# A gated attention block in fp32 accuracy: the start of the first group of heads reordered, the gated maximum taken from signed gates, six buffers for the factors of the product, the down weight in four pieces

## The chip, the core and the metric

The kernel runs on one core of a Trainium2 chip. The core has five engines with instruction streams of their own: PE (TensorE, matrix products into PSUM), DVE (VectorE), ACT (ScalarE), POOL (GpSimd) and SP (SyncE, which here issues nearly all DMAs). They meet only through semaphores. The metric is the device time of one execution in microseconds (us); lower is better.

## What is computed

x is (4, 1024, 512), the context of the same shape, all in fp32. The block is an attention of the normalized x over the context with 16 heads of 32 columns, then a feed-forward part whose activations and weights are quantized and dequantized (qdq). Cut to what matters:

```
q = rope(layernorm(x)); k = rope(ctx); v = ctx
scores = q k^T / sqrt(32) + slope[h] * (key - query)
x = x + tanh(g_xattn) * softmax(scores) v
h = act_qdq(layernorm(x))                       # 16 bits, one scale for the whole tensor
up = act_qdq(h @ lpbq(w_up).T); gate = act_qdq(h @ lpbq(w_gate).T)
gate = act_qdq(gate * u16_qdq(sigmoid(gate)))
x = x + tanh(g_ffn) * (act_qdq(gate * up) @ lpbq(w_down).T)
act_qdq(a): s = max|a| / 32767; round(a / s) * s
```

Each act_qdq needs the largest absolute value of the whole tensor before the first element can be quantized. So there are five such points: x, gate, gated gate, up, product.

## The kernel before, in words

**Attention.** The 64 pairs of batch and head are worked in 16 groups of four heads (p). A group has two halves of 512 queries (hf), and a half has 8 key tiles. `Step(g)` says what every engine does in step g; step g = 8 hf + kt. Row maxima run eleven steps ahead of the scores (`LEAD` 3 plus 8): a step takes two of them, each two 512-column matmuls on PE (L866) and one DVE reduction over 1024 columns (L1215). They need QA[p % 2] and KA[p % 2], the stacks of the high and low halves of queries and keys in 16 bits, with the position bias in rows 96 to 99. A stack is made so: ACT normalizes x (L1011), DVE or POOL applies rope, PE turns the tile (`turn`), ACT writes the high half `hi` (L1017), DVE the low half `lo` (L1229), SP stores both into DRAM (`store_parts`) and loads them from there in the layout of the stack (`load_stack`). For group 0 this stands ahead of everything. DVE first fills rows 96 to 127 of all four stacks (L1238, L1239), then takes the statistics of the first eight tiles of x (L1203). The eighth of them uses the buffer of the first (`NXL` 7), so its load waits for the first tile's statistics.

**Gate projection.** PE multiplies x_hl (high and low halves of the quantized x, one chunk `cp` of 1024 rows after the other) by Wg in 48 units `12 cp + ot` of 24 matmuls, 5.18 us each (the distance of two evictions). ACT evicts a unit into one of three buffers `ev` (L1111), DVE takes its largest absolute value (`largest`, L1451), SP stores it to DRAM. Beside that DVE and ACT prepare the x tiles of the next chunk (`low_x`, then SP's transposition `turn_x`, L655) and quantize the up and down weights (`wround`, `wsplit`, `wstore` in TILE_JOBS).

**Up projection.** 48 units with Wu, whose pieces SP loads by transposition, two for each four units (`load_wu`, some 2.7 us of SP for the two). Beside each unit ACT and DVE work through the gate chunks that `GATE_PLAN` gives to the step. Of the first kind there are 48: SP loads the chunk from DRAM (`load_gate`, three buffers gt), ACT quantizes it into gq (L1145) and takes the sigmoid (L1136), DVE rounds the sigmoid (L1487) and takes the largest |gq| * sigmoid (L1508); |gq| is written first into gab, by ACT (L1151) or DVE (L1505). Then the global maximum (`global_max`) gives the second scale. The second kind (`gated`: sigmoid again on ACT, rounding and product on DVE, L1493) rewrites gq. `LATE` of these are left for later. The down weight Wd[0] is loaded by one transposition in the 32nd step (L778).

**Products.** After the global maximum of up come 48 products of 1024 columns: SP loads up (`uf`, four buffers), ACT writes |up| quantized into uq (three buffers, L1163), ACT or DVE writes |gq| into pab (two buffers, L1171 on ACT for 33 of 48, L1534 on DVE for 15), DVE takes the largest product (L1537). The gated chunks that are left stand partly ahead of the products, partly between them. Wd[1] is loaded by one transposition behind the load for product 29 (L815). Then comes the down projection (L991), 1152 matmuls.

In the names of the profile, `ol` and `oh` are the memory in which pab and the products' operands lie.

Of the kernel before, what the change touches and what calls it, by code (L numbers as in the profile page):

```python
# [32 lines left out]
LATE = 14  # L33
# [71 lines left out]
class Step:  # L105


    def __init__(self, g):
# [11 lines left out]
        if w == 8 and 0 <= p and p + 2 < NQ:  # L120
            self.turn = (p + 2, 0)
        elif w == 0 and 0 <= p and p + 1 < NQ:
            self.turn = (p + 1, 1)
        elif g == -3:
            self.turn = (1, 0)
# [24 lines left out]
        elif g == -2:  # L150
# [79 lines left out]

def score_no(hf, kt, h):
# [32 lines left out]
ALL = 9  # L264
ALL_NO = {n: ALL * (k + 1) for k, n in enumerate(("w0", "x_row", "w1", "w2", "g_row", "h_row", "u_row", "o_row"))}
# [22 lines left out]
class Kernel:  # L288


    def __init__(self, nc, ctx, x, ctx_in, gx, gf, wg, wu, wd, cos_d, sin_d, id_d, bias_d, out):
# [35 lines left out]
        self.red = A("red", [128, 10], F32)  # L327
# [5 lines left out]
        self.mxg = A("mxg", [128, 48], F32)  # L333
# [66 lines left out]
        self.gab = [A(f"gab{i}", [128, GW], I16) for i in range(2)]  # L400
# [14 lines left out]
        self.prt = [self.ol[0][:, 4 * i:4 * i + 4, :].rearrange("p a n -> p (a n)").bitcast(F32) for i in range(2)]  # L415
        self.pab = [self.ol[1][:, 2 * i:2 * i + 2, :].rearrange("p a n -> p (a n)").bitcast(I16) for i in range(2)]
# [10 lines left out]
        self.d_st = [sem(f"d_st{i}") for i in range(2)]  # L427
        self.d_crow = [sem(f"d_crow{i}") for i in range(2)]
# [24 lines left out]
        self.a_sig, self.a_gab, self.a_uabs = sem("a_sig"), sem("a_gab"), sem("a_uabs")  # L453
# [8 lines left out]
        self.v_mx, self.v_sgq, self.v_gab, self.v_gmax = sem("v_mx"), sem("v_sgq"), sem("v_gab"), sem("v_gmax")  # L462
# [4 lines left out]
        self.g_ropek = sem("g_ropek")  # L467
# [41 lines left out]
def columns(p):  # L509
# [8 lines left out]
         "g_row", "g_v", "g_s", "g_r0", "g_r", "f2",  # L518
# [18 lines left out]
GAB_ON_ACT = [n % 12 in (0, 2, 5, 7, 10) for n in range(48)]  # L537
# [3 lines left out]
def gab_no(n):  # L541

    return sum(GAB_ON_ACT[i] == GAB_ON_ACT[n] for i in range(n + 1))

# [16 lines left out]
def sync_program(e, K):  # L561
# [19 lines left out]
    def store_parts(p, w):  # L581
        e.wait_ge(K.a_hi, turn_no(p, w, 1))
        if p >= 2:
            e.wait_ge(K.d_st[p % 2], 112 * (p // 2))
# [7 lines left out]
    def load_stack(p, w):  # L592
        if p >= 2:
            e.wait_ge(K.pe_score, score_no(2 * (p - 2) + 1, 7, 3))
        e.wait_ge(K.d_part[w], 32 * p + 32)
        if p == 0 and w == 0:
            e.wait_ge(K.v_aux, 4)
# [6 lines left out]
        if w == 0:  # L604
            if p == 0:
                e.wait_ge(K.d_bias, 48)
# [1189 lines left out]
```

## Time and profile before

| | us |
|---|---|
| median of 3 runs | 1931.48 (1930.20 to 1932.11) |
| the profiled execution | 1931.96 |
| its span, first to last instruction | 1930.2 |
| PE busy | 1681.3 (87%) |
| DVE busy | 1482.4 (77%) |
| ACT busy | 1189.2 (62%) |
| POOL busy | 809.6 (42%) |
| mean granted TensorE clock | 0.957 of full |

The chain of work that ended last spends 29% of the span on PE, nearly all in the two projection loops and the down projection. In the page's 40 slices (48 us each) PE is full from the third to the 32nd but for the 22nd, empty in the first and the 33rd and 34th, and full again to the end. A row of a timeline shows start, duration, engine, line, operation, and the idle time of that engine just before it with what ended it. A duration with xN goes from the start of the first of N instructions to the end of the last.

### The profile page before, as it was taken

The numbers are of one execution on the slowest core, as the hardware profiler recorded it, in microseconds if no ns is written. First come the engines' busy times: TensorE is split into PE (matmuls) and PEld (weight loads), VectorE is DVE, ScalarE is ACT, GpSimd is POOL, SyncE is SP. The second block draws the span as 40 slices with busy tenths as digits, with TensorE's granted clock in tenths as the row PEclk, the third lists the DMA queues.
The fourth block names the chain that finished last, engine by engine and source line by source line (L and its number), as shares of the span: only waits on it lengthen the run. The fifth ranks groups of instructions, "written<-read, shape, count | busy, mean of one in ns | idle before, by whom it ended". The sixth has DMA issues, their size and how long they took to land. (4 is left out here: it accounts for less than half of the span.)

```text
span 1930.2 us, 24973 instructions
## 1 busy us (share of the span) xinstructions
PE 1681.3 (87%) x8888; PEld 631.8 (33%) x8888; DVE 1482.4 (77%) x2113; ACT 1189.2 (62%) x1911; POOL 809.6 (42%) x442
## 2 busy tenths in 40 slices
PE   0899999999999999999975999999998900399999
PEld 0222333333333333333222444444443400044444
DVE  5889888888888887888855676549999998854451
ACT  2366677777777777776652332349996588854440
POOL 3488888978889888887620010200000000000000
PEclk9999999999999999999997999999999955699999
DMA  5478776657776667665356898759885268655452
GB/s 150 92 189 195 170 180 155 162 130 163 170 176 153 158 146 175 165 149 132 80 161 163 246 260 253 218 173 270 259 263 158 104 206 246 228 182 173 164 164 76
DMA packets 234396, 340.54 MB, mean 176 GB/s; under 512 B 73984, under 2 KB 153216, under 8 KB 226016
## 3 DMA queue, kind: packets, MB, share of 16 engines
q1 hardware_dynamic: 225344, 273.94, 48.2%
q0 software_dynamic: 8928, 65.02, 16.9%
q8 instruction: 70, 1.15, 0.2%
q14 instruction: 54, 0.44, 0.1%
HBM read 165.61 MB, written 93.45 MB: 134 GB/s over the span
## 5 line engine op out<-in xcount | busy, mean ns | idle before, releaser
L1033 ACT ACTIVATE P<-quad 128x512 f32<-128x512 f32 x1024 | 557.4, 599 | 223.1 <-PE quad L878 218.6
L1215 DVE TENSOR_REDUCE cm<-quad 128x1 f16<-128x1024 f32 x512 | 601.3, 1216 | 98.3 <-PE quad L866 97.1
L1721 POOL TENSOR_TENSOR Ps<-P,P 128x2048 f32<-128x2048 f32 x93 | 422.8, 4546 | 145.0 <-ACT P L1033 144.9
L878 PE MATMUL quad<-QA,KA 101*128 101x512 f16 x1024 | 352.4, 385 | 7.8 <-ACT P L1033 6.7
L866 PE MATMUL quad<-KA,QA 100*128 100x512 f16 x1024 | 328.9, 392 | 32.9 <-issue 12.9
L991 PE MATMUL quad<-Wd,oh 128*128 128x512 f16 x768 | 231.6, 382 | 131.8 <-DVE ol L1559 131.7
L914 PE MATMUL quad<-P,cg 128*32 128x512 f32 x2048 | 273.6, 606 | 3.6 <-ACT numT L1064 0.6
L960 PE MATMUL quad<-x_hl,Wg 128*128 128x512 f16 x1152 | 251.5, 382 | 22.2 <-DMA x_hl<-xs 22.2
L960 PE MATMUL quad<-x_hl,Wu 128*128 128x512 f16 x1152 | 251.5, 381 | 6.4 <-DMA Wu<-wt_scratch 6.4
L1111 ACT ACTIVATE ev<-quad 128x1024 f32<-128x1024 f32 x96 | 97.5, 1016 | 201.4 <-PE quad L960 196.6
L1451 DVE TENSOR_REDUCE mxt<-ev 128x1 f32<-128x1024 f32 x96 | 116.9, 1217 | 95.9 <-ACT ev L1111 95.5
L878 PEld LDWEIGHTS quad<-QA,KA 101*128 101x128 f16 x1024 | 85.9, 97 | 299.7 <-ACT P L1033 209.2
L960 PEld LDWEIGHTS quad<-x_hl,Wg 128*128 128x128 f16 x1152 | 113.2, 98 | 160.3 <-issue 26.1
L960 PEld LDWEIGHTS quad<-x_hl,Wu 128*128 128x128 f16 x1152 | 113.0, 98 | 144.7 <-DMA Wu<-wt_scratch 7.4
L866 PEld LDWEIGHTS quad<-KA,QA 100*128 100x128 f16 x1024 | 98.6, 98 | 180.1 <-DVE cm L1215 41.2
L991 PEld LDWEIGHTS quad<-Wd,oh 128*128 128x128 f16 x768 | 75.4, 98 | 227.8 <-issue 130.9
L991 PE MATMUL quad<-Wd,ol 128*128 128x512 f16 x384 | 146.5, 382 | 0.0
L1697 POOL TENSOR_TENSOR wq<-wl,wsc 128x512 f32<-128x512 f32 x36 | 37.9, 1052 | 218.8 <-DVE wl L1326 218.8
L1136 ACT ACTIVATE sgm<-gq,qs 128x1024 f32<-128x1024 int16 x96 | 109.3, 1145 | 26.5 <-DVE sgq L1487 24.0
L1581 DVE SCALAR_TENSOR_TENSOR xr<-quad,qs,xr 128x512 f32<-128x512 f32 x32 | 24.0, 751 | 122.6 <-PE quad L991 122.6
L944 PE MATMUL quad<-Ps,ones 128*32 128x512 f32 x776 | 101.0, 592 | 1.8 <-DMA Ps<-P 1.5
L1180 ACT ACTIVATE uq<-uf,qs 128x512 int16<-128x512 f32 x96 | 68.2, 711 | 53.0 <-DMA uf<-up_scratch 51.5
(140 smaller groups left out, 1841.1 us busy)
## 6 DMA issues: line engine op xcount, KB each, us to landing
Ps<-P POOLq DMA_DIRECT2D x62, 1024.0 KB, 8.1
gate_scratch<-ev SPq DMA_DIRECT2D x48, 512.0 KB, 3.0
gt<-gate_scratch SPq DMA_DIRECT2D x48, 512.0 KB, 5.7
up_scratch<-ev SPq DMA_DIRECT2D x48, 512.0 KB, 3.1
uf<-up_scratch SPq DMA_DIRECT2D x48, 512.0 KB, 4.8
uf<-up_scratch SPq DMA_DIRECT2D x96, 256.0 KB, 3.8
KA<-part_scratch SPq DMA_DIRECT2D x48, 256.0 KB
QA<-part_scratch SPq DMA_DIRECT2D x48, 256.0 KB
```

What stands on the lines that cost most here:

```text
L866: mm = e.matmul(K.bank(use, c), K.QA[p % 2][0:100, qc, h, q0:q0 + 128], K.KA[p % 2][0:100, h, 512 * c:512 * c + 512], start=True, stop=True)
L878: e.matmul(K.score[h % 2], K.KA[p % 2][0:101, h, 128 * kt:128 * kt + 128], K.QA[p % 2][0:101, qc, h, :], start=True, stop=True).then_inc(K ...
L914: mm = e.matmul(K.num[32 * h:32 * h + 32, :], K.cg[p % 3][:, kt, 32 * h:32 * h + 32], K.Pb[before.g % NP][:, h, :], start=kt == 0, stop=kt ...
L944: mm = e.matmul(K.den[32 * h:32 * h + 32, :], K.ones[:, :], K.Ps[n % 2 if hf == NHALF - 1 else n][:, h, :], start=n == 0, stop=n == (3 if ...
L960: mm = e.matmul(K.quad[z][:, 512 * h:512 * h + 512], W(part, c), K.x_hl[:, x, c0:c0 + 512], start=n == 0, stop=n == 11)
L991: mm = e.matmul(ps, o[k][:, ot, sl], K.Wd[r][:, ot, :], start=m == 0, stop=m == 3 * OT - 1)
L1033: e.activation(K.Pb[pb][:, h, :], K.score[h % 2], ACT.Exp, scale=SCALE / (QPOW * KPOW)).then_inc(K.a_exp, 1)
L1111: e.activation(K.ev[k % NEV][:, :], K.quad[k % 4][:, :], ACT.Copy).then_inc(K.a_ev, 1)
L1136: e.activation(K.sgm[n % NSG][:, :], view(n), ACT.Sigmoid, scale=sg).then_inc(K.a_sig, 1)
L1215: e.tensor_reduce(cm[:, u:u + 1], K.quad[UNIT["max", hm, u] % 2][:, :], AX.X, ALU.max).then_inc(K.v_max, 1)
L1451: e.tensor_reduce(K.mxt[:, col:col + 1], K.ev[k % NEV][:, :], AX.X, ALU.max, apply_absolute_value=True).then_inc(K.v_mx, 1)
L1721: e.tensor_tensor(K.Ps[n][:, :, :], K.Pb[(st.g - 1) % NP][:, :, :], K.Pb[st.g % NP][:, :, :], ALU.add).then_inc(K.g_sum, 1)
```

## The change

Four edits:

1. **Start.** Rows 96 to 127 of KA[0] and QA[0] are filled by ACT, those of KA[1] and QA[1] by DVE later, behind the low halves of keys and queries. The key turn of group 0 is split on ACT and DVE ahead of the normalization. Its halves don't go through DRAM: 12 DMAs of 32 partitions copy keys from hi and lo into KA[0], 12 more the queries, with a semaphore for each head. The turn and the store of group 1's queries stand four steps earlier (g = -7 and -6 instead of -3 and -2).
2. **Gated maximum.** gab and its 48 copies go. DVE multiplies gq itself with scale -1, so that it finds the largest product of the negative gates; the positive side is taken from the largest signed gate, which a second reduction per unit of the gate projection gives (`highest`) with a second global maximum `s_row`. GATE_PLAN puts the 48 gates into 25 steps instead of 28 and 40 of the gated chunks instead of 34 into steps 26 to 46; `LATE` is 8 instead of 14.
3. **Products.** Six buffers for pab and for |up| (`uqa`) instead of two and three. ACT's copy for product n + 5 is issued behind the operand of product n.
4. **Down weight.** Wd[0] is loaded in four pieces, one in each of the last four groups of four units, behind the second store of the group; Wd[1] in four pieces at the place where the one load stood.

```diff
-LATE = 14
+LATE = 8
+NUA = 6
...
-        elif g == -3:
+        elif g == -7:
             self.turn = (1, 0)
...
-        elif g == -2:
+        elif g == -6:
             self.store_parts = (1, 0)
...
-        until = 48 * step // 28 if step <= 28 else 48 + (48 - LATE) * (step - 28) // 20
+        until = 48 * step // 25 if step <= 25 else 48 + (48 - LATE) * min(step - 25, 21) // 21
...
-    return range(48 - LATE, 52 - LATE), {n: 52 - LATE + n // 2 for n in range(48) if n % 2 == 1 and 52 - LATE + n // 2 < 48}
+    return range(48 - LATE, 50 - LATE), {2 * i + 1: 50 - LATE + i for i in range(LATE - 2)}
...
+    def first_keys():
+        e.wait_ge(K.v_lo, 2)
+        for h in range(4):
+            for n, src in enumerate((K.hi[1], K.lo[1], K.hi[1])):
+                e.dma_start(K.KA[0][32 * n:32 * n + 32, h, :], src[32 * h:32 * h + 32, :]).then_inc(K.d_first_k, 16)
+        e.wait_ge(K.a_aux, 2)
+        e.wait_ge(K.d_bias, 48)
...
+    def first_queries():
+        e.wait_ge(K.v_lo, 4)
+        for h in range(4):
+            for n, src in enumerate((K.hi[0], K.hi[0], K.lo[0])):
+                dst = K.QA[0][32 * n:32 * n + 32, :, h, :]
+                e.dma_start(dst, src[32 * h:32 * h + 32, :].rearrange("d (c t) -> d c t", c=2)).then_inc(K.d_first_q[h], 16)
...
-    store_parts(0, 1)
-    store_parts(0, 0)
-    load_stack(0, 1)
-    load_stack(0, 0)
+    first_keys()
+    first_queries()
...
+    def load_wd(part, j):
...
+        rows = slice(128 * j, 128 * j + 128)
+        e.dma_start_transpose(K.Wd[part][:, :, rows], K.wt_d[2][part][rows, :]).then_inc(K.d_Wd, 16)
...
+    e.wait_ge(K.a_tg, 1)
+    for rows, value in ((K.KA[0][96:128, :, :], -1.0), (K.QA[0][96:128, :, :, :].rearrange("p c h t -> p (c h) t"), QPOW * KPOW)):
+        some = K.tg[96:128, 0:1].to_broadcast([32, rows.shape[1] * rows.shape[2]]).rearrange("p (a t) -> p a t", a=rows.shape[1])
+        e.activation(rows, some, ACT.Copy, scale=0.0, bias=value).then_inc(K.a_aux, 1)
+    turned(0, 1, 0)
+    turned(0, 1, 1)
     normalize(0, 0, 8)
...
+    def gate_abs(n):
+        if PAB_ON_ACT[n]:
+            e.wait_ge(K.v_g2, n + 1)
+            if n >= NUA:
+                e.wait_ge(K.v_pmax, n - NUA + 1)
+            e.activation(K.pab[n % NUA], view(n), ACT.Abs).then_inc(K.a_pab, 1)
...
-        e.activation(K.uq[n % NUQ][:, :], K.uf[uf_uses % NUF][:, :], ACT.Abs, scale=ru).then_inc(K.a_uabs, 1)
+        e.activation(K.uqa[n % NUA], K.uf[uf_uses % NUF][:, :], ACT.Abs, scale=ru).then_inc(K.a_uabs, 1)
         uf_uses += 1
         if n in beside:
             sigmoid(beside[n], 48 + beside[n])
...
+        if n + NUA - 1 < 48:
+            gate_abs(n + NUA - 1)
...
+    def highest(k, col):
+
+        e.tensor_reduce(K.mxs[:, col:col + 1], K.ev[k % NEV][:, :], AX.X, ALU.max).then_inc(K.v_mx, 1)
...
-                    e.tensor_tensor_reduce(out=K.sgm[k][:, :], in0=K.gab[z][:, :], in1=K.sgq[k][:, :], scale=1.0, scalar=0.0, op0=ALU.mult,
+
+                    e.tensor_tensor_reduce(out=K.sgm[k][:, :], in0=view(n), in1=K.sgq[k][:, :], scale=-1.0, scalar=0.0, op0=ALU.mult,
```

**What moved on SP at the start.** Before, behind the load of the second group's x:

```order
L675 DMA bias_scratch<-biash_100 32x1024
L587 DMA part_scratch<-hi_144 128x1024
L589 DMA part_scratch<-lo_146 128x1024
L587 DMA part_scratch<-hi_143 128x2x512
L589 DMA part_scratch<-lo_145 128x2x512
L603 DMA KA_91<-part_scratch 32x4x1024 x3
L603 DMA QA_89<-part_scratch 32x8x512 x3
L608 DMA KA_91<-bias_scratch 4x4096
```

Now, at the same place; the copies of the other heads are alike and stand between:

```order
L702 DMA bias_scratch<-biash_104 32x1024
L624 DMA KA_95<-hi_148 32x1024
L624 DMA KA_95<-lo_150 32x1024
...
L628 DMA KA_95<-bias_scratch 4x4096
L635 DMA QA_93<-hi_147 32x2x512 x2
L635 DMA QA_93<-lo_149 32x2x512
```

The four stores into part_scratch are gone, and each head has three copies of its own for keys and three for queries.

**What moved on ACT in the up projection.** Four steps before, each begun by an eviction into ev:

```order
L1111 ACTIVATE ev_165<-quad 128x1024
L1145 ACTIVATE gq<-gt_172,qs 128x1024
L1136 ACTIVATE sgm_174<-gq,qs 128x1024
L1151 ACTIVATE gab_178<-gq 128x1024
L1111 ACTIVATE ev_163<-quad 128x1024
L1145 ACTIVATE gq<-gt_170,qs 128x1024
L1136 ACTIVATE sgm_173<-gq,qs 128x1024
L1145 ACTIVATE gq<-gt_171,qs 128x1024
L1136 ACTIVATE sgm_174<-gq,qs 128x1024
L1151 ACTIVATE gab_178<-gq 128x1024
L1111 ACTIVATE ev_164<-quad 128x1024
```

Now:

```order
L1158 ACTIVATE ev_169<-quad 128x1024
L1192 ACTIVATE gq<-gt_176,qs 128x1024
L1183 ACTIVATE sgm_177<-gq,qs 128x1024
L1192 ACTIVATE gq<-gt_174,qs 128x1024
L1183 ACTIVATE sgm_178<-gq,qs 128x1024
L1158 ACTIVATE ev_167<-quad 128x1024
```

The copies gab are gone, and nearly every step has two gates (gq, sgm), where before steps with one and with two alternated.

**What moved on ACT in the products.** Before, at the first products (uq is |up|, ol is |gq|, sgm a gated chunk's sigmoid):

```order
L1163 ACTIVATE uq_185<-uf_181,qs 128x1024
L1171 ACTIVATE ol_191<-gq 128x1024
L1163 ACTIVATE uq_186<-uf_182,qs 128x1024
L1136 ACTIVATE sgm_173<-gq,qs 128x1024
L1163 ACTIVATE uq_187<-uf_183,qs 128x1024
L1171 ACTIVATE ol_191<-gq 128x1024
```

Now (|up| is oh):

```order
L1222 ACTIVATE oh_190<-uf_186,qs 128x1024
L1183 ACTIVATE sgm_178<-gq,qs 128x1024
L1208 ACTIVATE ol_192<-gq 128x1024
L1222 ACTIVATE oh_190<-uf_183,qs 128x1024
L1208 ACTIVATE ol_192<-gq 128x1024
L1222 ACTIVATE oh_190<-uf_184,qs 128x1024
```

The copy of |gq| stands behind the sigmoid, and it is that of five products later.

## Rows read from the trace of the kernel before

**Rows 1.** Window: us, busy and (instructions) by engine, PEclk, DMA share, GB/s.

```profile
1300.00:1400.00 100.00, 100.00 (x465) 45.34 (x463) 96.43 (x127) 95.07 (x92) 0.00 (x0) 1.00 0.88 262
```

**Rows 2.** Timeline of the start, all engines.

```profile
9.09 1.05 ACT L1047 ACTIVATE biash<-bias 32x1024 f16<-32x1024 f32 x1 [2.70 <-DMA bias<-in_alibi_dram]
...
14.48 3.47 DVE L1239 MEMSET QA<- 32x4096 f16 x1 [0.80 <-issue]
...
18.03 0.67 DVE L1203 BATCH_NORM_STATS2 st<-xl 128x6 f32<-128x512 f32 x1
...
24.40 1.18 DVE L1245 TENSOR_TENSOR biash<-bias,biash 32x1024 f16<-32x1024 f32 x1
...
29.44 3.18 ACT L1011 ACTIVATE xn<-xg,nm,rs 128x128 f32<-128x128 f32 x8 [19.30 <-POOL nm L1637]
...
39.11 0.69 DVE L1229 SCALAR_TENSOR_TENSOR lo<-quad,hi 128x512 f16<-128x512 f32 x1 [0.16 <-ACT hi L1017]
...
52.44 10.65 DVE L1215 TENSOR_REDUCE cm<-quad 128x1 f16<-128x1024 f32 x9 [12.63 <-PE quad L866]
```

**Rows 3.** DMA issues, 0 to 60 us: count, KB each, median us to landing.

```profile
xl<-in_x_dram SPq DMA_DIRECT2D x8, 256.0 KB, 6.7
...
part_scratch<-hi SPq DMA_DIRECT2D x2, 256.0 KB, 2.1
```

**Rows 4.** Gate projection: DVE's reduction by line, one unit's window, SP's timeline.

```profile
L1451 DVE TENSOR_REDUCE mxt<-ev 128x1 f32<-128x1024 f32 x47 | 57.3, 1220 | 88.5 <-ACT ev L1111 88.5
...
1127.48:1132.72 5.24, 5.24 (x26) 2.36 (x25) 4.45 (x8) 2.13 (x3) 1.05 (x1) 1.00 1.05 247
...
1156.73 1.84 SPq L655 DMA_TRANSPOSE x_hl<-xs  x1
```

**Rows 5.** Up projection: timeline; waits on and landing of the gate loads.

```profile
1284.54 45.70 PE L960 MATMUL quad<-x_hl,Wu 128*128 128x512 f16 x211
...
1290.50 1.02 ACT L1111 ACTIVATE ev<-quad 128x1024 f32<-128x1024 f32 x1 [4.74 <-DVE qs L1423]
...
1302.63 1.00 ACT L1111 ACTIVATE ev<-quad 128x1024 f32<-128x1024 f32 x1
...
1304.07 1.21 SPq L761 DMA_DIRECT2D gt<-gate_scratch  x2
...
1305.91 1.13 ACT L1145 ACTIVATE gq<-gt,qs 128x1024 int16<-128x1024 f32 x1
...
1308.14 1.00 ACT L1111 ACTIVATE ev<-quad 128x1024 f32<-128x1024 f32 x1
...
  DMA gt<-gate_scratch: 6.6, 9
...
DMA to landing us min/median/max: 4.4/5.7/6.7
```

**Rows 6.** Timeline of the later up projection, DVE and PE.

```profile
1455.42 0.19 DVE L1409 TENSOR_REDUCE red<-mxg 128x1 f32<-128x48 f32 x1
...
1464.57 1.28 DVE L1493 SCALAR_TENSOR_TENSOR gq<-sgq,qs,gq 128x1024 int16<-128x1024 uint16 x1
...
1469.54 1.28 DVE L1493 SCALAR_TENSOR_TENSOR gq<-sgq,qs,gq 128x1024 int16<-128x1024 uint16 x1
...
1477.94 7.33 PE L960 MATMUL quad<-x_hl,Wu 128*128 128x512 f16 x23 [5.38 <-DMA Wu<-wt_scratch]
...
1548.54 0.19 DVE L1409 TENSOR_REDUCE red<-mxt 128x1 f32<-128x48 f32 x1
```

**Rows 7.** Timeline of the products, DVE and SP.

```profile
1559.56 1.22 DVE L1537 CUSTOM_DVE_ANT_0 ol<-uq,ol 128x1024 f32<-128x1024 int16 x1
...
1616.50 1.22 DVE L1537 CUSTOM_DVE_ANT_0 ol<-uq,ol 128x1024 f32<-128x1024 int16 x1
...
1617.36 8.65 SPq L815 DMA_TRANSPOSE Wd<-wt_scratch  x1
...
1665.94 0.20 DVE L1409 TENSOR_REDUCE red<-mxt 128x1 f32<-128x48 f32 x1
```

More of the change, by code:

```diff
@@ L536, with mx_no @@
 GATE_PLAN = gate_plan()
-GAB_ON_ACT = [n % 12 in (0, 2, 5, 7, 10) for n in range(48)]
 PAB_ON_ACT = [n % 16 * 11 % 16 < 11 for n in range(48)]
-def gab_no(n):
-    return sum(GAB_ON_ACT[i] == GAB_ON_ACT[n] for i in range(n + 1))
+def mx_no(k):
+    return 2 * k + 2 if k < 48 else 49 + k
 def pab_no(n):
@@ L761, in load_gate @@
         e.dma_start(K.gt[n % NGT][:, :], K.gate_d[ot, :, GW * cp:GW * cp + GW]).then_inc(K.d_gt[n % NGT], 16)
+    def load_wd(part, j):
+        if part == j == 0:
+            e.wait_ge(K.a_gq, 48)
+            for h in range(2):
+                for i in range(2):
+                    e.wait_ge(K.d_wh[h][i], 16 * 18)
+        rows = slice(128 * j, 128 * j + 128)
+        e.dma_start_transpose(K.Wd[part][:, :, rows], K.wt_d[2][part][rows, :]).then_inc(K.d_Wd, 16)
     load_gate(0)
@@ L772, in sync_program @@
                     load_gate(n + 2)
[L773 to L778 removed]
+            if cp == 1 and ot >= 8:
+                load_wd(0, ot - 8)
     uf_uses = [0]
@@ L814, in sync_program @@
             e.wait_ge(K.v_g2, 48)
-            e.dma_start_transpose(K.Wd[1][:, :, :], K.wt_d[2][1]).then_inc(K.d_Wd, 16)
+            for j in range(4):
+                load_wd(1, j)
     for n in range(NUF - 1):
@@ L1014, in turned @@
         e.wait_ge(K.pe_turn, turn_no(p, w, half))
-        if p > 0 and half == 0:
-            e.wait_ge(K.d_part[w], 32 * p)
+        if p == 1 and half == 0:
+            if w:
+                e.wait_ge(K.d_first_k, 208)
+            else:
+                for h in range(4):
+                    e.wait_ge(K.d_first_q[h], 48)
+        elif p > 1 and half == 0:
+            e.wait_ge(K.d_part[w], 32 * p - 32)
         e.activation(K.hi[w][:, 512 * half:512 * half + 512], K.bank(("turn", p, w), half), ACT.Copy, scale=(QPOW, KPOW)[w]).then_inc(K.a_hi, 1)
@@ L1047, in scalar_program @@
     e.activation(K.biash[0][:, :], K.bias[:, :], ACT.Copy).then_inc(K.a_bias, 1)
+    e.wait_ge(K.a_tg, 1)
[4 more added lines that the diff above has]
+    turned(0, 1, 1)
     normalize(0, 0, 8)
-    for w in (1, 0):
-        for half in range(2):
-            turned(0, w, half)
+    turned(0, 0, 0)
+    turned(0, 0, 1)
     for st in STEPS:
@@ L1156, in scalar_program @@
         sigmoid(n, 48 + n)
+    e.wait_ge(K.pe_prj, 96)
+    for n in range(NUA - 1):
+        gate_abs(n)
     e.wait_ge(K.v_q, Q_NO["u_r"])
@@ L1226, in low_part @@
         e.wait_ge(K.a_hi, turn_no(p, w, half))
-        if p > 0 and half == 0:
-            e.wait_ge(K.d_part[w], 32 * p)
+        if p == 1 and half == 0:
+            if w:
+                e.wait_ge(K.d_first_k, 208)
+            else:
+                for h in range(4):
+                    e.wait_ge(K.d_first_q[h], 48)
+        elif p > 1 and half == 0:
+            e.wait_ge(K.d_part[w], 32 * p - 32)
         e.scalar_tensor_tensor(K.lo[w][:, c], K.bank(("turn", p, w), half), (QPOW, KPOW)[w], K.hi[w][:, c], ALU.mult, ALU.subtract).then_inc(K.v_lo, 1)
@@ L1259, in vector_program @@
     e.tensor_tensor(K.t1[0][:, :, :], K.t1[0][:, :, :], K.t2[:, :, :], ALU.add).then_inc(K.v_rope0, 1)
-    for w in (1, 0):
-        for half in range(2):
-            low_part(0, w, half)
+    low_part(0, 0, 0)
+    low_part(0, 0, 1)
+    e.memset(K.QA[1][96:128, :, :, :], QPOW * KPOW).then_inc(K.v_aux, 1)
     def everywhere(out, column, name):
```

115 lines of the change are left out of this document (60 added, 55 removed).

## The prediction

> **What bounds the kernel now.** I read first the busy time of all engines in windows, then the timeline of the places that the change touches, in the order of the program.
>
> From 100 us to 1542 us TensorE is the bound but for short gaps. In the up projection ScalarE and VectorE are close behind it: from 1300 to 1400 us PE is busy 100 of 100 us, DVE 96.4 and ACT 95.1 [rows 1]. Two stretches have no TensorE work to hide in. One is the start: the first row maximum is taken at 52.44 us after 12.6 us in which DVE waited for it [rows 2]. The other is the product stage, from the global maximum of the up projection at 1548.54 [rows 6] to that of the products at 1665.94 [rows 7], 117.4 us, in which DVE is the fullest engine. What is saved at the start moves everything behind it; so does what is saved in the product stage. In between a saving counts only as far as the engine that is late next allows.
>
> **Part 1, the start.** Now the chain is: four fills by DVE of 3.47 us each, the last from 14.48; statistics of eight x tiles from 18.03, done at 24.4; nine small operations on POOL; eight normalizations on ACT at 29.44; rope, turn, split, whose last half ends at 39.11 + 0.69 = 39.80; stores to DRAM; loads of KA and QA from there; first maximum at 52.44 [rows 2].
>
> The fills leave the head of DVE's queue: two go to ACT, two behind other work. ACT ends its bias copy at 10.1 (1.05 us for 1024 columns [rows 2]); an estimate from that row for two fills of 4096 columns is 2 x 4.2 = 8.4 us, until 18.6, and ACT isn't needed by this chain before the key turn at about 19. The statistics can follow the arrival of the tiles: the eighth tile's load waits for the first tile's statistics, which moves from 18.7 to about 12, and a tile lands 6.7 us after issue [rows 3]. So the statistics end at about 18.3 (bounds: 16.5, where the other loads have drained; 20.5, if this one comes last behind all) in place of 24.4. Everything up to the last split follows at the distances it has now: 39.8 - 6.1 = 33.7. In it the key split (1.3 us) and one fill (3.5) that now stand on DVE ahead of rope hide behind POOL and ACT: DVE is free at about 25, rope starts at 26.6. What would uncover them is statistics that end 1.6 us earlier still.
>
> Then the trip through DRAM goes: instead of stores, three large loads each and 12.6 us, there are 12 small transfers for the keys, issued at 21 to 26, and 12 for the queries. Only the first head's three count: 3 issues of 0.4, landing 2.1 us after issue as the stores of hi do [rows 3], 1.0 for the matmuls: 33.7 + 1.2 + 2.1 + 1.0 = 38.0. The other heads are due every 4 x 1.18 us and come every 1.3. The last fill on DVE ends at 33.7 + 3.5 + 0.8 = 38.0: just hidden. So the first maximum comes at 38.0 instead of 52.44: **-14.4 us** (bounds -9 to -16; the far end takes 6.7 us for a landing, as the x tiles have). The second group's turn stands four steps earlier, behind ten maxima at about 50; POOL has its rope ready at 36 + 7.3 = 43, so it costs there what it costs now. I expect the rest of attention to move as a block.
>
> A page speaks against it: the Trainium skill, "SBUF — State Buffer", section "Door 1: The DMA port swizzle", says that a transfer on 32 partitions reaches 8 of the 16 ports, half the rate, and no row here shows such a transfer of this size. By its 436 GB/s the first head's 192 KB would take 0.9 us instead of 0.45, and the sum would be -13.9 instead of -14.4.
>
> **Part 2, the gate projection.** It gains 48 reductions on DVE of 1.22 us [rows 4] in units of 5.18 us of TensorE. Where the weights of the up projection and the x tiles meet, seven units in a row hold 4.45 us of DVE work [rows 4]; with 1.2 more that is 5.65, 0.47 too much each, 3.3 us of lag after seven. The eviction doesn't feel it, its buffer is three units deep. The last x tile of the third chunk does: its low half and the split of the weights behind it come 3.3 + 1.2 us later, at 1157.5. SP stores that split, issues two weight loads (1.9) and a projection (0.4) before it can issue the tile's transposition, which stands at 1156.73 now [rows 4] and goes to about 1160.2: 3.5 late, and TensorE takes the chunk 3.6 us after it now without a wait, so I give it no slack. The same place a chunk later has one load instead of two: 1.8 late. Sum **+5** (bounds 0, if landings leave slack, to +9, if TensorE comes back at 1.2 GHz, as after the 5.4 us gap at 1477.94, where 23 matmuls took 7.3 us [rows 6]).
>
> **Part 3, the up projection.** The first eviction waits for the gate scale, 1.2 later behind the 48th new reduction: 1290.5 [rows 5] to 1291.7; the second maximum (2.5 us) comes behind it and is hidden. The copies of the absolute gate go: 28 on DVE, 20 on ACT. The plan now puts 48 gates in 25 steps instead of 28. On ACT a step with two gates is 0.9 for the eviction and 2 x 2.2 (1305.91 to 1308.14 [rows 5]): 5.35, near TensorE's 5.18. But a loop stands over it. The load of a gate is issued behind the eviction two steps ahead of the next one: from 1302.63 to 1304.07, 1.44 us, then 5.7 us to landing (4.4 to 6.7; the ones that ACT waited for are nearer to 5.9) [rows 5], then two gates, 4.4: 11.8 us for two steps, against 10.4 of TensorE. Twelve such pairs, less 2.2 twice at the two steps with one gate, are 137 us: step 25 at 1428.8. Two gates more (7.2) and a reduction (1.2), and the gated maximum is looked for at 1437.2 instead of 1455.42 [rows 6]. Its chain is 3.4 us, with the three operations on the top value 4.0. Then 40 gated chunks and 22 reductions follow on DVE. Two chunks and one reduction take 4.97 (1464.57 to 1469.54 [rows 6]): 20 x 4.97 + 2 x 1.2 = 101.8. End: 1437.2 + 4.0 + 101.8 = 1543.0 instead of 1548.54: **-5.6 us**. TensorE could be done by 1284.5 [rows 5] + 48 x 5.18 = 1533.2, with 2.5 for evicting and reducing 1536; so DVE is late next. The gap of 5.38 us at 1477.94, where SP put the whole down weight ahead of a piece of the up weight [rows 6], goes, since a quarter now stands behind a store with 20 us to spare; but it frees only TensorE, and isn't counted again. A lag of ACT over about 11 us at a fourth step makes TensorE wait for the next weight; by the sum above the lag is 10 to 12 there, so 0 to 3 us of waits, which DVE hides. Bounds: landings of 5.3 give TensorE's limit, -13; of 6.7, 12 x 0.8 more, +4.
>
> **Part 4, the products.** Two gated chunks instead of four stand ahead of the first product: -3.9. Six instead of ten stand among the products. Now the 24 products from 1559.56 to 1616.50 take 56.9 us [rows 7], DVE without a gap. With the change DVE's own work in the first twelve is 12 x 1.15 + 4 x 1.26 + 6 x 1.92 = 30.4, but the six buffers do not free ACT: it now makes the copy for product n + 5 right behind the operand of n, and that copy's buffer is free only when product n - 1 is done. Behind it stand the next operand and sigmoid, for which DVE waits. That serial piece is 1.0 + 1.0 + 1.1 on ACT, 0.7 + 1.2 + 1.2 on DVE, 6.2 us and hand-overs, for two products, where ACT makes the copy, and 4.2 to 5 where DVE does. I take 5.7 a pair, 34 us, and 12 x 1.8 for the next twelve: 56 against 56.9, -1. From the 24th on ACT bounds both, with 1.7 a product; the stall behind the second down weight (SP busy 8.65 us [rows 7]) stays, since the four pieces follow each other with no load between: one piece is three up weight pieces (1.3 each) less what is fixed, about 2.3, 9.2 in all, +0.6. Sum **-4** (bounds -12, if the operands run free as DVE's own work allows, to +2).
>
> **Sum.** -14.4 + 5 - 5.6 - 4 = -19.0. Against the profiled execution's own 1931.96 us (span 1930.2) this is 1913.0; the median of the runs stands 0.5 below that execution, so I say 1912.5.
>
> **Rivals.** *TensorE's limit*: the gate loads land sooner than DVE needs, and the up projection gives -13: 1905. For it: landings go down to 4.4. Against: nine of 48 gates already wait for their load, at 1.7 a step [rows 5]. The Trainium skill, "DMA: Bandwidth & Descriptors", section "Anatomy of one DMA", gives about 2.0 us plus bytes by 436 GB/s, 3.2 us for these 512 KB, by which this rival would be the outcome; the trace has 5.7 beside other transfers, and that I use. *Small transfers are slow*: the query pieces land like the x tiles and the start gives -8: 1919. *The products run free*: -12 there, 1904.5. *The new reductions drag*: more lag in the gate projection, clock lost, +12 instead of +5: 1919.5. *The change doesn't do what it says*: six buffers bring nothing; this is in my forecast. *Slower than before*: the tighter plan makes the gate loads collide with the stores of the up projection. Each us of landing costs 12 in the first 25 steps; from 7.5 us all of the gain is gone, at 8.4 the kernel stands at 1942. Against: 6.7 is the longest now, and bytes per us rise only by a tenth.
>
> **Chances.** Forecast (1907 to 1917) 0.5; TensorE's limit 0.15; slow small transfers 0.12; reductions drag 0.1; products free 0.1; slower 0.03. The range 1901 to 1923 leaves out the last and the rest of the far bounds. Less than 0.2% (3.9 us) can't be told from no change; to end there two of the parts must fail at once: 0.03. Faster 0.94, slower 0.03.
>
> **What would show it.** The first reduction of a score tile at about 38 us. In the gate projection TensorE waiting at the third and fourth chunk for x_hl. In the up projection ACT waiting for the gate loads in most steps, 11.6 to 12 us per two steps, and the gated maximum near 1437, counted from the same start of that stage. DVE without a gap from there. In the product stage DVE waiting for ACT among the first twelve. Wrong it would be if part 1's shift does not reach the end of attention, or if the landings move by over 0.7 us.

## The result

The changed kernel takes 1908.78 us (median of 4 runs, 1905.94 to 1910.37), the kernel before 1931.80 (4 runs, 1930.20 to 1933.05). The ratio is 0.988, 95% interval 0.9863 to 0.9897: 23.0 us faster, where 19.0 was forecast. The profiled execution of the changed kernel took 1908.31 us, its span is 1906.5.

Cut at the same instructions, the two profiles differ as follows (us). The first five rows add up to the span.

| stage, from ... to ... | before | after | difference | forecast |
|---|---|---|---|---|
| start, to the first row maximum | 52.4 | 38.3 | -14.1 | -14.4 |
| attention, to the first matmul of the gate projection | 980.7 | 980.8 | 0 | 0 |
| gate projection, to the first matmul with Wu | 251.4 | 253.7 | +2.3 | +5 |
| up projection, to its global maximum | 264.0 | 255.6 | -8.4 | -5.6 |
| products, to their global maximum; then the down projection | 117.4; 264.3 | 113.9; 264.2 | -3.5; 0 | -4; 0 |
| of the up projection: to the gated maximum | 170.9 | 150.3 | -20.6 | -18.2 |

The start, timeline of the changed kernel, against [rows 2]:

```profile
10.24 3.61 ACT L1093 ACTIVATE KA<-tg 32x4096 f16<-32x4096 f32 x1
10.42 0.69 DVE L1259 BATCH_NORM_STATS2 st<-xl 128x6 f32<-128x512 f32 x1 [9.50 <-DMA xl<-in_x_dram]
...
18.16 1.18 DVE L1304 TENSOR_TENSOR biash<-bias,biash 32x1024 f16<-32x1024 f32 x1
...
32.87 0.69 DVE L1291 SCALAR_TENSOR_TENSOR lo<-quad,hi 128x512 f16<-128x512 f32 x1 [0.16 <-ACT hi L1058]
33.59 1.32 SPq L635 DMA_DIRECT2D QA<-hi  x2
...
34.95 0.60 SPq L635 DMA_DIRECT2D QA<-lo  x1
...
37.27 1.86 PE L901 MATMUL quad<-KA,QA 100*128 100x512 f16 x4 [5.07 <-DMA QA<-lo]
...
38.32 2.36 DVE L1271 TENSOR_REDUCE cm<-quad 128x1 f16<-128x1024 f32 x2 [0.38 <-PE quad L901]
```

The statistics end 6.2 us earlier (18.16 for 24.40), the last split ends at 33.56 for 39.80, and from there the first row maximum takes 4.8 us in place of 12.6.

The gate projection: the 30 us that end 0.15 us behind the start of the third chunk's last transposition as a window (busy and count of PE, PEld, DVE, ACT, POOL; PEclk, DMA share, GB/s), first in the kernel before, then in the changed one:

```profile
1126.88:1156.88 30.00, 30.00 (x141) 13.60 (x139) 23.31 (x38) 11.68 (x16) 5.24 (x5) 1.00 0.94 264
...
1115.08:1145.08 30.00, 30.00 (x140) 13.58 (x139) 29.68 (x43) 11.99 (x16) 5.24 (x5) 1.00 0.88 248
```

SP's and PE's timelines of the changed kernel, against [rows 4]:

```profile
1144.93 1.77 SPq L682 DMA_TRANSPOSE x_hl<-xs  x1
...
1150.46 62.32 PE L995 MATMUL quad<-x_hl,Wg 128*128 128x512 f16 x288 [1.31 <-DMA x_hl<-xs]
1213.19 57.14 PE L995 MATMUL quad<-x_hl,Wg 128*128 128x512 f16 x264 [0.41 <-DMA x_hl<-xs]
```

DVE is busy 29.7 of these 30 us; in the kernel before it was 23.3. TensorE waits twice, at the third and the fourth chunk; in the kernel before it waits for nothing in the whole stage.

The up projection: the window of [rows 1] (its start lies 27 us behind the stage's start, and there 15), PE's and DVE's timelines, and the loads of the gates, against [rows 5, 6]:

```profile
1300.00:1400.00 100.00, 100.00 (x465) 45.35 (x464) 87.12 (x122) 92.56 (x88) 0.00 (x0) 1.00 0.97 288
```

```profile
1272.76 27.57 PE L995 MATMUL quad<-x_hl,Wu 128*128 128x512 f16 x127
...
1423.08 0.20 DVE L1471 TENSOR_REDUCE red<-mxg 128x1 f32<-128x49 f32 x1
...
1528.40 0.20 DVE L1471 TENSOR_REDUCE red<-mxt 128x1 f32<-128x48 f32 x1
```

```profile
  DMA gt<-gate_scratch: 7.0, 11
...
DMA to landing us min/median/max: 4.5/5.5/7.1
```

DVE is busy 87 of 100 us in place of 96 (the copies of the absolute gate are gone), and TensorE waits for nothing in this profile of the stage. From the gated maximum to the end of the stage DVE is busy 103.4 of 105.3 us: it is late, not TensorE, whose last matmul of the stage starts at 1521.2.

The products, timeline and ACT's two groups of the stage (out<-in, count | busy, mean ns | idle before, releaser), against [rows 7]:

```profile
1535.58 1.22 DVE L1608 CUSTOM_DVE_ANT_0 ol<-oh,ol 128x1024 f32<-128x1024 int16 x1
...
1592.55 1.23 DVE L1608 CUSTOM_DVE_ANT_0 ol<-oh,ol 128x1024 f32<-128x1024 int16 x1 [0.24 <-issue]
...
1593.85 9.99 SPq L795 DMA_TRANSPOSE Wd<-wt_scratch  x4
...
1642.30 0.20 DVE L1471 TENSOR_REDUCE red<-mxt 128x1 f32<-128x48 f32 x1
```

```profile
L1222 ACT ACTIVATE oh<-uf,qs 128x1024 int16<-128x1024 f32 x48 | 53.6, 1135 | 12.5 <-DMA uf<-up_scratch 9.5 <-DVE qs L1485 3.0
L1208 ACT ACTIVATE ol<-gq 128x1024 int16<-128x1024 int16 x33 | 34.4, 1048 | 12.4 <-DVE mxt L1608 12.2
```

The first product comes 7.2 us after the stage's start, where it was 11.0. The next 24 take 57.0 us in place of 56.9. The copies of |gq| on ACT (L1208) waited 12.2 us for a product.

### The profile page after: what moved, and what is told of

Its sections match the earlier page's. It is cut to its first block and busy times, and to the rows that moved or that the text cites. A ratio compares the mean times of both kernels' runs of the same rounds, so it can differ in the third digit from the quotient of the medians.

```text
span 1906.5 us, 24960 instructions
## 1 busy us (share of the span) xinstructions
PE 1679.1 (88%) x8888; PEld 631.9 (33%) x8888; DVE 1502.7 (79%) x2143; ACT 1182.9 (62%) x1895; POOL 809.8 (42%) x442
```

## The experiments

Each kernel was timed against the kernel before on the same chip. A stage's length comes from the kernel's one profile. "Up" is the up projection to its global maximum, "products" the stage behind it, "tail" the time from TensorE's last matmul with Wu to the maximum of the products (the loads of up values can't begin before that matmul).

| kernel | median us | ratio (95% interval) | gate proj. | gated max. | up | products | tail |
|---|---|---|---|---|---|---|---|
| before | 1931.8 | | 251.4 | 170.9 | 264.0 | 117.4 | 123.9 |
| changed | 1908.8 | 0.988 (0.9863 to 0.9897) | 253.7 | 150.3 | 255.6 | 113.9 | 121.1 |
| e1_start | 1918.0 | 0.9942 (0.9928 to 0.9957) | 251.4 | 172.0 | 264.5 | 116.4 | 122.8 |
| e2_fills | 1925.1 | 0.9976 (0.9964 to 0.9987) | 251.4 | 169.9 | 262.3 | 115.6 | 122.0 |
| e3_no_signed | 1906.9 | 0.988 (0.9863 to 0.9896) | 251.3 | 152.7 | 258.0 | 115.1 | 120.8 |
| e4_ahead4 | 1903.2 | 0.9871 (0.9852 to 0.989) | 253.8 | 155.3 | 260.6 | 106.2 | 114.5 |
| e5_spread | 1904.0 | 0.9857 (0.9842 to 0.9872) | 253.2 | 152.6 | 257.9 | 108.5 | 116.0 |
| e6_ngt4 | 1905.3 | 0.9869 (0.9855 to 0.9884) | 253.6 | 141.9 | 251.2 | 116.7 | 119.4 |
| e7_wd0 | 1907.1 | 0.9878 (0.9862 to 0.9895) | 253.6 | 152.4 | 257.6 | 113.9 | 119.7 |
| e8_old_buffers | 1904.7 | 0.9862 (0.9847 to 0.9877) | 253.0 | 155.2 | 260.4 | 108.0 | 115.7 |
| e9_combo | 1891.1 | 0.9801 (0.9784 to 0.9819) | 253.9 | 141.8 | 251.2 | 102.6 | 105.3 |
| e10_late4 | 1888.9 | 0.9789 (0.9774 to 0.9803) | 253.1 | 142.9 | 257.0 | 96.8 | 105.4 |
| e11_early | 1890.1 | 0.9797 (0.978 to 0.9813) | 253.9 | 143.0 | 257.1 | 94.9 | 103.5 |
| e12_late6 | 1890.7 | 0.9786 (0.9772 to 0.98) | 253.6 | 143.4 | 253.7 | 100.0 | 105.2 |

Two columns measure how far one profile can be trusted. The up projection has the same code in the changed kernel, e4, e5, e7 and e8, and takes 255.6, 260.6, 257.9, 257.6 and 260.4: what varies is how soon the gate loads land. ACT waited for them 7.0, 12.0, 8.9, 9.1 and 11.8 us, and each length less its wait is 248.5 to 249.0. Attention takes 977.9 to 981.7 in all fourteen profiles. So a difference of 2 us in a stage is read only where the stage itself repeats, as the gate projection and the down projection (264.2 to 264.6) do.

The whole times say less. The interval of the changed kernel overlaps those of e3 to e8, so each of these six differs from it only in the length of its stages. Of the kernels that start from the changed one, e9 to e12 alone are faster than it as a whole.

### The start alone

```diff
-    store_parts(0, 1)
-    store_parts(0, 0)
-    load_stack(0, 1)
-    load_stack(0, 0)
+    first_keys()
+    first_queries()
...
-        elif g == -3:
+        elif g == -7:
             self.turn = (1, 0)
```

This one has the whole first edit (the fills, the order of steps, the direct copies, the turn), and nothing else of the change.

> The kernel before with the reordering of the first group's steps alone (fills, key and query steps, direct copies in place of the trip through DRAM, the second group's turn four steps earlier). The whole of it is computed. Theory (attention moves as a block): the first row maximum at 38.3 us, the first matmul of the gate projection at 1033.16 - 14.1 = 1019.1, every later stage as long as before, so 1931.8 - 14.1 = 1917.7. Rival (the shift is partly eaten by work that did not move, POOL's or a transfer's): the first maximum at 38.3, but the gate projection starts later than 1021, and the whole gains less than 12.

Measured: 1917.95 us, the first maximum at 38.3, the gate projection's first matmul at 1020.0, later stages as before. Against the kernel before on this chip (1930.42) that is 12.5 us by the medians, 8.3 to 13.9 by the ratio's interval, whose end lies just short of 14.1; the spans of the two profiles differ by 13.6, since attention took 0.9 longer in this one, which is within its scatter. No later stage took anything of it systematically: what is saved at the start is saved at the end, within 1 to 3 us.

### The fills and the order without the direct copies

```diff
-        e.memset(K.KA[i][96:128, :, :], -1.0).then_inc(K.v_aux, 1)
-        e.memset(K.QA[i][96:128, :, :, :], QPOW * KPOW).then_inc(K.v_aux, 1)
...
+        e.activation(rows, some, ACT.Copy, scale=0.0, bias=value).then_inc(K.a_aux, 1)
```

> The kernel before with only the fills and the order of steps of the first group changed; the trip through DRAM and the second group's turn stay as before. Theory (the two gains of the start are separate): the last split ends at 33.6 in place of 39.8, the trip takes its 12.6 us as before, the first maximum at 46.2, and the whole is 1931.8 - 6.2 = 1925.6. Rival (the trip was set by something that did not move, such as the bias rows or the loads of other tiles on the same queue): the first maximum later than 48, and a gain under 4.5.

Measured: 1925.06 us, 5.4 below the kernel before on the same chip (2.5 to 7.0 by the interval). Its timeline at the same place as that of the changed kernel above:

```profile
33.66 0.37 SPq L589 DMA_DIRECT2D part_scratch<-lo  x1
...
45.16 1.86 PE L868 MATMUL quad<-KA,QA 100*128 100x512 f16 x4 [12.89 <-issue]
...
46.21 4.71 DVE L1223 TENSOR_REDUCE cm<-quad 128x1 f16<-128x1024 f32 x4 [8.20 <-PE quad L868]
```

The last split ends at 33.63, the trip takes its 12.6 us, the maximum comes at 46.2. So the 14.1 us are two gains that add: 6.2 from the head of DVE's queue, 7.9 from the trip.

### No signed reductions

```diff
-            highest(u, 4 * ot + cp)
...
-    global_max(K.mxs[:, :], "s_row")
+    global_max(K.mxt[:, :], "s_row")
```

> The changed kernel without its 48 signed reductions in the gate projection; the top gate is taken from the largest absolute value instead, so the scale of the gated values can differ. The gate projection takes 253.7 us in the changed kernel and 251.4 in the one before. Theory (the reductions hold back the split of the last x tiles of the third and fourth chunk): without them the two short waits for x_hl go, the stage takes 251.4 again, and the whole is 1908.8 - 2.3 = 1906.5. Rival (the waits come from transfers, which stand otherwise since the stage starts earlier): they stay, the stage takes 253 or more, and the whole is within 0.7 of the changed kernel.

Measured: the gate projection takes 251.3 us again, and the whole 1906.88; the ratio is that of the changed kernel, 0.988, so the whole time can't show the 2.3 us, and the stage does. The ten kernels with the reductions stand at 253.0 to 253.9, the four without them (before, e1 and e2 too) at 251.3 to 251.4. So some 2.3 us are the reductions' price. Its timeline shows no wait at the third and the fourth chunk any more. (A wait of 1.18 us for x_hl that it does show stands at 1022.95, five microseconds into the stage, and others have the like.)

### Copies four products ahead

```diff
-    for n in range(NUA - 1):
+    for n in range(NUA - 2):
         gate_abs(n)
...
-        if n + NUA - 1 < 48:
-            gate_abs(n + NUA - 1)
+        if n + NUA - 2 < 48:
+            gate_abs(n + NUA - 2)
```

> The changed kernel with one number changed: ScalarE makes the absolute copy four products ahead instead of five, so the buffer it writes is that of product n - 2, not of the product just being computed. Theory (the copy waits for the product before it, 12.2 us of ACT in the stage, and six buffers bring nothing for that reason): the waits go, the stage of 113.9 us (from the global maximum of the up projection to that of the products) takes about 105, and the whole is about 1900. Rival (the loads of the up values or DVE's own work set the pace there): ACT's waits move to the loads, the stage takes 111 or more and the whole 1906 or more.

The chain that this experiment is to break, timeline of the changed kernel, seventh and eighth product:

```profile
1551.68 1.22 DVE L1608 CUSTOM_DVE_ANT_0 ol<-oh,ol 128x1024 f32<-128x1024 int16 x1
1551.86 1.06 ACT L1208 ACTIVATE ol<-gq 128x1024 int16<-128x1024 int16 x1 [2.24 <-DVE mxt L1608]
1552.82 1.13 ACT L1222 ACTIVATE oh<-uf,qs 128x1024 int16<-128x1024 f32 x1
...
1553.86 1.13 ACT L1183 ACTIVATE sgm<-gq,qs 128x1024 f32<-128x1024 int16 x1
...
1555.02 0.69 DVE L1555 TENSOR_SCALAR sgq<-sgm 128x1024 uint16<-128x1024 f32 x1 [2.11 <-ACT sgm L1183]
1555.75 1.28 DVE L1561 SCALAR_TENSOR_TENSOR gq<-sgq,qs,gq 128x1024 int16<-128x1024 uint16 x1
...
1558.21 1.22 DVE L1608 CUSTOM_DVE_ANT_0 ol<-oh,ol 128x1024 f32<-128x1024 int16 x1
```

ACT's copy waits 2.24 us until a product is done; the next operand and the sigmoid stand behind it; DVE waits 2.11 for the sigmoid. From one product to the next 6.5 us pass in which each engine waits for the other once; with the copies four ahead the same distance is 4.3. This is the longest of three such places in the first twelve products; the other two cost 0.9 us each. In the kernel with the copies four ahead ACT's group of copies reads:

```profile
L1208 ACT ACTIVATE ol<-gq 128x1024 int16<-128x1024 int16 x33 | 34.3, 1044 | 4.7 <-DVE mxt L1608 4.7
```

Measured: the wait falls from 12.2 to 4.7 us, the stage takes 106.2 in place of 113.9 (105 expected), the first 24 products 50.3 us in place of 57.0. The whole is 1903.20, 3 above the expectation, and the ratio, 0.9871, can't be told from the changed kernel's 0.988. Part of the reason may be what the profile has: the longest up projection of its kind, 260.6, in which ACT waited 12.0 us for gate loads. The rival, which had the loads as the limit, is out: ACT's wait for them went from 9.5 to 10.1 us only.

### The second down weight in pieces that are apart

```diff
-        if n == 26:
-            e.wait_ge(K.v_g2, 48)
-            for j in range(4):
-                load_wd(1, j)
+        if n in (20, 24, 28, 32):
+            if n == 20:
+                e.wait_ge(K.v_g2, 48)
+            load_wd(1, (n - 20) // 4)
```

> The changed kernel with the four pieces of the second down weight put four products apart (behind the loads at products 20, 24, 28 and 32) instead of all at product 26. Theory (the block of 10 us on SP leaves ACT without its up values for about 8 us, and one piece of 2.5 us fits between loads that run three ahead): no wait over 2 us for a load in the stage, which takes 113.9 - 6 = 108, the whole about 1903. Rival (ACT's wait for its own copy buffer takes back what the loads give): the stage takes 111 or more. If the pieces themselves disturb the loads of the up values, it takes 114 or more.

Measured: 108.5 us for the stage, 1903.98 for the whole. ACT's operands:

```profile
L1222 ACT ACTIVATE oh<-uf,qs 128x1024 int16<-128x1024 f32 x48 | 53.5, 1135 | 7.4 <-DMA uf<-up_scratch 4.4 <-DVE qs L1485 3.0
```

The wait for loads falls from 9.5 to 4.4 us, the stage by 5.4. Cutting the load in four, as the change does, gives nothing here as long as the pieces follow each other: SP is busy with them 9.99 us in place of 8.65 [rows 7], and ACT's longest wait for an up value behind them is 6.5 us in place of 6.0. Only apart do they pay.

### Four gate buffers

```diff
-NGT, NSG = 3, 2
+NGT, NSG = 4, 2
...
-                if n + 2 < 48:
-                    load_gate(n + 2)
+                if n + 3 < 48:
+                    load_gate(n + 3)
```

> The changed kernel with four buffers for the gate values instead of three and their loads issued three ahead. Theory (the loop eviction, store, load, landing, two gates sets the first 25 steps of the up projection): ACT's waits for gates (7.0 us in 11 times, in the sister runs up to 12.0) shrink under 3; ACT's own 5.35 a step sets the pace, the gated maximum comes 138 to 142 us after the stage's start instead of 150 to 155, and the stage ends near TensorE's limit, at 251 to 252 instead of 255.6 to 260.6: the whole about 1904. Rival (ACT and DVE hold each other by the two sigmoid buffers, loads only fill the slack): the gated maximum stays above 148.

DVE's timeline, and the loads of the gates:

```profile
1412.80 0.20 DVE L1472 TENSOR_REDUCE red<-mxg 128x1 f32<-128x49 f32 x1
```

```profile
DMA to landing us min/median/max: 4.8/6.3/8.1
```

Measured: no wait of ACT for a gate load is left, though the loads land later than before (6.3 for 5.5 us). The gated maximum comes 141.9 us after the stage's start, the stage takes 251.2, 2.7 behind TensorE's last matmul. That is the rival "TensorE's limit" of the prediction, made to happen: the loop over landings had set the pace. But the whole gains less than the 4.4 us of this stage, since the products start earlier and the loads of up values don't: their stage is 2.8 longer, and the tail only 1.7 shorter.

### The first down weight in one piece

```diff
-            if cp == 1 and ot >= 8:
-                load_wd(0, ot - 8)
+            if 4 * ot + cp + 1 == 32:
...
+                e.dma_start_transpose(K.Wd[0][:, :, :], K.wt_d[2][0]).then_inc(K.d_Wd, 16)
```

> The changed kernel with the first down weight loaded in one piece at step 32 of the up projection, as before the change; the second stays in four pieces. Theory (its gap frees only TensorE, since DVE is late next): TensorE waits about 5 us for a piece of the up weight, its last matmul of the stage comes up to 5 later than 248.4 us after the start, the global maximum of the up projection stays within 1.5 of 255.6 to 260.6, and the whole within 1.5 of the changed kernel. Rival (TensorE's end carries through): the maximum 4 to 5 later, the whole 1913.

Measured: up 257.6 us, whole 1907.14: within 1.7 us of the changed kernel's whole, and no slower (ratios 0.9878 and 0.988). The price on TensorE was missed:

```profile
1448.76 6.63 SPq L812 DMA_TRANSPOSE Wd<-wt_scratch  x1
...
1459.58 62.33 PE L999 MATMUL quad<-x_hl,Wu 128*128 128x512 f16 x288 [1.70 <-DMA Wu<-wt_scratch]
```

TensorE waits 1.70 us and not 5.38 [rows 6]. SP spends 6.63 us on the weight in both, but here begins at 1448.76, 9.1 before TensorE would have needed the piece of Wu; before the change it began at 1467.14, 5.4 ahead of that. So the four pieces of the first down weight bring nothing that can be measured.

### The products with the buffers of before

```diff
-        if n + NUA - 1 < 48:
-            gate_abs(n + NUA - 1)
+        if PAB_ON_ACT[n]:
+            e.wait_ge(K.v_g2, n + 1)
+            if n >= 2:
+                e.wait_ge(K.v_pmax, n - 1)
+            e.activation(K.pab[n % 2], view(n), ACT.Abs).then_inc(K.a_pab, 1)
```

> The changed kernel with the product stage's buffers and order of copies as before the change (two for the copy of the absolute gated value, made behind its own operand, three for the operand), everything else as changed, with 8 late chunks. Theory (six buffers bring nothing, the 3.5 us gained in this stage come from the fewer late chunks): the stage takes 113 to 115 us, as the changed kernel's 113.9 and 115.1. Rival (the six buffers carry the gain): 117 or more.

ACT's copies of |gq|:

```profile
L1219 ACT ACTIVATE ol<-gq 128x1024 int16<-128x1024 int16 x33 | 34.5, 1044 | 3.3 <-DVE mxt L1598 3.3
```

Measured: 108.0 us for the stage and 1904.72 for the whole. Neither expectation holds. The six buffers as the change uses them don't bring nothing, they cost 5.9 us of the stage, and without them the stage is 9.4 shorter than before (117.4 to 108.0). These 9.4 are the fewer late chunks, and whatever the four pieces of the second weight do to them. With two buffers the copy made beside product n waits for product n - 2, 3.3 us in all; with six and made five ahead, the copy that stands there waits for n - 1, 12.2 us. So the price is that of the lookahead and not of the buffers: with the same six and the copies four ahead (e4) the stage takes 106.2, 1.8 less than with two, a difference that is too small to be read from one profile each.

### Together, and the last late chunks

e9_combo has the edits of e4, e5 and e6 at once.

> The changed kernel with the three edits together: copies four products ahead, the second down weight in pieces four products apart, four gate buffers. Theory (the three take away different waits and add): the up projection from its first matmul to its global maximum 251 to 252 us, the product stage 113.9 - 7.7 - 5.4 = 101, plus 3 because the loads of the up values can't start before TensorE ends: 104, the whole 1908.8 - 4 - 10 = 1895. Rival (one resource, DVE's or ACT's own work, stands behind both waits of the product stage): the stage takes 106 or more, as with the copies alone, and the whole is 1899 or more.

Measured: products 102.6, up 251.2, whole 1891.06, ratio 0.9801: the three add. The kernel before took 1929.0 on this chip, so the ratio is the fair measure: it is worth 38.4 us of 1931.8, where 36.8 were expected. The next one changes the plan too:

```diff
-LATE = 8
+LATE = 4
...
-        until = 48 * step // 25 if step <= 25 else 48 + (48 - LATE) * min(step - 25, 21) // 21
+        until = 2 * step if step <= 24 else 48 + (48 - LATE) * min(step - 24, 22) // 22
```

> The kernel with the three edits, and a plan of 24 steps with two gates each, 44 gated chunks in the 22 steps behind, 4 late chunks instead of 8. Theory (with the gates in time, ACT's 5.35 us a step sets the gated maximum at 135 to 137 us after the stage's start, and DVE's 2.48 a chunk fits the rest: 136 + 4 + 22 x 4.97 = 249): the up projection still takes 251 to 253, and the product stage 4 to 6 less than with 8 late chunks: the whole about 1890. Rival (the loads or ACT fall behind the tighter plan): the up projection takes 255 or more and what the product stage gives is gone.

Measured: the products gain 5.8 as expected, but the gated maximum doesn't come sooner: it stands at 142.9 us. ACT's last sigmoid ends at 139.5, behind two waits for gate loads (1.9 us together), and the last gates' way through DVE, which the sum of the expectation had left out, takes 3.4 more. The up projection takes 257.0 and not 251 to 253. The tail is the same, 105.4. Then the loads of the first up values ahead of the last stores:

```diff
     for k in range(NEV):
-        e.wait_ge(K.d_ev[k], 16 * 32)
+        e.wait_ge(K.d_ev[k], 16 * 31)
     e.wait_ge(K.pe_prj, 96)
```

> As the one with 4 late chunks, and the first three loads of up values are issued as soon as TensorE is done, without waiting for the last three stores to land; DVE waits for these ahead of its first product. Theory (ACT stands for its first up value behind the scale, and the loads start about 3.5 us earlier): the time from TensorE's last up matmul to the maximum of the products falls by 3, the whole about 1887. Rival (the scale's chain on DVE ends as late as the loads land): within 1 of the kernel without it.

Measured: a tail of 103.5, 1.9 less where 3 was expected; the whole can't be told from the one without it. And this kernel with 6 late chunks:

> The kernel with all edits and the early loads, with 6 late chunks in place of 4. With 8 the up projection ends at 251.2 us after its start and the product stage takes 102.6; with 4 it is 257.1 and 94.8. Theory (each late chunk costs DVE 1.97 us in whichever stage stands on it, and about two chunks still fit beside TensorE): the up projection 252 to 254, the product stage 97 to 99, from TensorE's last up matmul to the maximum of the products 101.5 instead of 103.5, the whole about 1887. Rival (the late chunks cost the same in both stages): 103 to 105, the whole as the other two, 1889 to 1891.

Measured: 253.7 and 100.0, a tail of 105.2 (103.5 with four): not the theory, and near the rival. From e9 to e10 four chunks cost the up projection 5.9 us and spared the products 5.8, as much in one stage as in the other; from four chunks to six (e11 to e12) the up projection gave 3.4 and the products took 5.2, so that nothing was won by the middle. The four kernels e9 to e12 can't be told apart (ratios 0.9786 to 0.9801, intervals that overlap); all four are faster than the kernel before and than the changed one, whose interval begins at 0.9863.

## Why the prediction was right, and where not

**The start** was right in its steps: statistics at 18.2 (18.3), last split 33.6 (33.7), three issues, landing, 38.3 (38.0); e2_fills shows the two gains apart. Of the way from the split to the maximum, 4.8 us for 4.3, the third copy is issued 1.4 behind the split (1.2 for three issues, but one takes 0.6 and not 0.4), lands 2.0 later (2.1), and the matmuls and their hand-overs take 1.3 (1.0). The prediction's estimate from the Trainium skill, "SBUF — State Buffer", section "Door 1: The DMA port swizzle", was -13.9 for this part against the forecast's -14.4; with -14.1 the trace decides for neither.

**The gate projection** had the right mechanism and place (the third and fourth chunk wait for x_hl) and the wrong size, +2.3 for +5. Two terms were mis-sized. The first is the lateness. In the kernel before DVE takes the maximum of each of the seven units of the second chunk in question 0.03 us behind the eviction. In the changed kernel it does so 0.35, 0.67, 1.02, 1.33, 1.65, 1.97 and 2.28 us behind: a lag of 0.32 a unit where 0.47 was put, 2.3 after seven and not 3.3. The last split of the weights is 3.6 late for 4.5, the transposition, put 3.5 late, stands at 1144.93 where 1142.65 would be on time (1156.73 less the start's 14.08), 2.3 late. The second is the slack, put at nothing: in the kernel before the last tile landed at 1161.62, 1.2 us ahead of the first matmul that reads it, the chunk's 13th at 1162.81. So TensorE waited 1.31 at the third chunk, and 0.41 at the fourth, for which 1.8 had been put. The clock gave nothing away. The stage's first 8 us, behind TensorE's idle 22 us, have a granted clock of 0.63 (0.66 in the kernel before), and every window behind them has 1.00, that around the wait of 1.31 us too; in the kernel before, the 7.3 us behind the gap of 5.38 have 0.70. So the far end of +9 was out.

**The up projection**: the loop was right. The gated maximum was put 152.7 us after the stage's start; the profile has 150.3, the four sisters with the same code 152.4 to 155.3. The forecast for the stage was 258.5; the five profiles have a median of 257.9. So of the 2.8 us by which this term fell short of the profile, 2.3 are the spread of the loads' landings. e6_ngt4 shows that the loop was the cause. ACT waited for its loads less often than the prediction looked for, 11 times in 25 steps and not in most. DVE was late next, as said, and TensorE's gap brought nothing (e7_wd0). By the fit in the section "Anatomy of one DMA" of the Trainium skill's page "DMA: Bandwidth & Descriptors", which the page gives for transfers that GpSimd issues, a gate load was estimated at 3.2 us; SP issues these loads, no landing of them was below 3.9, and the medians were 5.5 to 6.3, so the outcome that the prediction drew from the page, TensorE's limit, did not come by itself.

**The products** came out right in sum (-3.5 for -4) with a wrong account. The serial piece was there as described: the first twelve products take 34.4 us (forecast 34), and with the copies four ahead 30.3, which is DVE's own work (30.4). But the comparison behind "-1" was made with the kernel before, in which ten chunks stand among the products. Against the old order with six, 51.6 us for 24 products in e8_old_buffers, the new order's 57.0 is a loss. The step that failed is "six buffers bring nothing": with the copies five ahead they took away more than half of the 9.4 us that the rest of the change gave. That the terms of this part (-3.9, -1, +0.6) come near what was measured (-3.8, 0.0, +0.3) shows that the stalls were priced well, and not that the new order was worth making.

**The sum** of medians of like profiles is -14.1 + 2.2 - 6.1 - 2.5 = -20.5 (gate projection, up projection and products taken as the median of the profiles with the same code: before, e1 and e2; the changed kernel and its sisters). The measured 23.0 has an interval of 19.9 to 26.5, which holds this sum; the forecast's 19.0 stands 0.9 outside it.

## What to carry to other kernels

More buffers help only if the engine that fills them doesn't ask for the one that is in use: with k buffers, a fill that runs k - 1 items ahead waits for the item that the consumer has in hand, and whatever stands behind the fill on that engine waits too; one item less of lookahead was worth 7.7 us of the stage. A long transfer cut in pieces gains when the pieces stand apart between the loads that they would delay, and not by the cutting. When a sum comes out right, undo its parts one by one: two of them may have opposite signs.

## What the hardware showed that was not expected

- A fill of 32 partitions by 4096 elements takes ACT 3.59 to 3.61 us as a copy with scale zero, about what DVE's memset takes (3.47), and not the 4.2 scaled up from its copy of 1024 columns.
- SP spends 0.58 to 0.68 us on the issue of a copy of 64 KB from one SBUF tile to 32 partitions of another, and 0.34 to 0.37 on a store of 256 KB from a split at the start; the small copies of the queries land in 2.0 to 2.1 us, the stores in 2.0 to 2.2.
- The landing of the same 48 gate loads of 512 KB goes from 3.9 to 9.3 us over the runs, and this moves the up projection by up to 5 us between profiles with the same code in that stage, while the down projection repeats within 0.4.
